# A graph network in one kernel: in the two relation passes, each row's three bf16 parts added up in PSUM by three narrow products instead of side by side by one wide one

## The reference, cut to what matters

```python
def _rgcn_conv(x, src, dst, edge_type, inv_deg, basis, comp, root, bias):
    xs = x[src]
    c = comp[edge_type]
    m = c[:, 0:1] * (xs @ basis[0])
    for b in range(1, basis.shape[0]):
        m = m + c[:, b:b + 1] * (xs @ basis[b])
    agg = jax.ops.segment_sum(m * inv_deg[:, None], dst, num_segments=n_nodes)
    return agg + x @ root + bias
...
deg = jnp.zeros((n_rel, n_nodes), jnp.float32).at[edge_type, dst].add(1.0)
inv_deg = 1.0 / jnp.maximum(deg[edge_type, dst], 1.0)
...
h = relu(_rgcn_conv(x, ..., basis1, comp1, root1, bias1))
return _rgcn_conv(h, ..., basis2, comp2, root2, bias2)
```

## Time and profile before

| | |
|---|---|
| median of 3 runs | 5605.86 us (5604.53 to 5606.44) |
| span of the profiled execution | 5606.0 us |
| instructions | 259126 |
| TensorE products busy | 4652.9 us, 83% |
| VectorE busy | 4578.9 us, 82% |
| ScalarE busy | 2971.1 us, 53% |
| first and second relation pass | about 905 and 897 us |
| granted TensorE clock, mean | 0.911 |

### The profile page before, as it was taken

The page is one execution under the profiler, slowest core; times in us unless marked ns, Lnnn a source line. Parts: engine busy times, 40 slices in busy tenths (PEclk is TensorE's granted clock), DMA queues, the critical chain, the costliest instruction groups (busy, mean ns, idle before and its releaser), DMA issues.

```text
span 5606.0 us, 259126 instructions
## 1 busy us (share of the span) xinstructions
PE 4652.9 (83%) x99331; PEld 3864.3 (69%) x99331; DVE 4578.9 (82%) x10121; ACT 2971.1 (53%) x9016; POOL 1075.8 (19%) x1785
## 2 busy tenths in 40 slices
PE   2566666666399999977996999979999998999998
PEld 1344433444299999977886999967777776777776
DVE  8999999999799999988888888886666666666665
ACT  2566656666132222227775333346666665666665
POOL 2455555555211111110000222210000000000000
PEclk7777777777699999988998999989999999999999
DMA  1000000000188888850001444433333333333332
GB/s 47 1 1 1 1 1 1 1 1 1 48 260 255 253 253 253 254 161 13 0 0 45 121 121 121 120 90 91 89 90 90 89 90 87 91 91 91 90 90 78
DMA packets 305217, 501.31 MB, mean 89 GB/s; under 512 B 76918, under 2 KB 78454, under 8 KB 305126
## 3 DMA queue, kind: packets, MB, share of 16 engines
q1 hardware_dynamic: 303782, 499.39, 30.7%
q0 software_dynamic: 576, 0.52, 0.0%
q10 hardware_dynamic: 768, 0.16, 0.0%
HBM read 408.40 MB, written 91.57 MB: 89 GB/s over the span
## 4 chain that ended last, share of the span: by engine, by line
PE 47%; DVE 27%; issue 17%; ACT 3%; POOL 3%; DVEq 1%; DMA 1%; ACTq 0%; POOLq 0%; another core or an unknown queue 0%; SPq 0%
PE PS L1415 17%; PE PS L1408 8%; DVE agg L1764 7%; PE PS L1211 6%; DVE arena L1728 5%; PE PS L1189 4%; PE PS L1191 4%; DVE Hp L1728 3%; DVE arena L1770 2%; POOL arena L737 2%; DVE tmp L1728 2%; ACT arena L971 2%; PE PS L1462 2%; PE PS L1206 2%; PE PS L1445 1%
## 5 line engine op out<-in xcount | busy, mean ns | idle before, releaser
L1728 DVE TENSOR_TENSOR arena<-iotab,arena 128x1024 bf16<-128x1024 bf16 (+6 forms) x1813 | 1741.5, 990 | 452.9 <-PE PS L1415 383.9
L971 ACT ACTIVATE arena<-PS 128x384 bf16<-128x384 f32 x2450 | 1069.2, 495 | 601.5 <-PE PS L1408 598.4
L1415 PE MATMUL PS<-arena 32*128 32x193 bf16 (+1 forms) x41552 | 1082.1, 243 | 7.6 <-issue 3.4
L808 ACT ACTIVATE arena<-PS,m 128x196 bf16<-128x196 f32 x1813 | 746.0, 431 | 547.3 <-POOLq L570 328.8
L1415 PEld LDWEIGHTS PS<-arena 32*128 32x128 bf16 x41552 | 815.8, 93 | 198.5 <-issue 166.1
L1077 PE MATMUL PS<-arena,tmp 128*128 128x262 bf16 x1813 | 504.7, 327 | 294.6 <-DVE tmp L1728 294.4
L1408 PE MATMUL PS<-Hp,arena 128*128 128x192 bf16 (+1 forms) x4900 | 644.4, 250 | 91.1 <-DVE Hp L1575 34.9
L1069 PE MATMUL PS<-agg,onesb 128*128 128x196 bf16 x1715 | 513.4, 301 | 202.9 <-ACT arena L808 198.5
L1070 PE MATMUL PS<-Hp,own_b 128*128 128x196 bf16 x1813 | 544.4, 304 | 55.8 <-DVE Hp L1728 54.5
L1408 PEld LDWEIGHTS PS<-Hp,arena 128*128 128x128 bf16 x4900 | 338.4, 99 | 304.5 <-issue 178.7
L1189 PE MATMUL PS<-Hp,arena 128*128 128x72 bf16 x7350 | 499.3, 198 | 44.0 <-DVE arena L2094 40.8
(11 more groups left out here) (362 smaller groups left out, 8170.2 us busy)
## 6 DMA issues: line engine op xcount, KB each, us to landing
arena<-hots SPq DMA_DIRECT2D x735, 256.0 KB, 2.6
arena<-codes SPq DMA_DIRECT2D x245, 512.0 KB, 5.2
hots<-arena SPq DMA_DIRECT2D x245, 256.0 KB, 5.2
arena<-hots SPq DMA_DIRECT2D x147, 320.0 KB
arena<-codes SPq DMA_DIRECT2D x49, 640.0 KB, 5.6
hots<-arena SPq DMA_DIRECT2D x49, 320.0 KB, 5.5
rows_h<-Hn SPq DMA_DIRECT2D x4, 1568.0 KB, 9.1
rows_l<-Y SPq DMA_DIRECT2D x1, 1764.0 KB, 10.4
```

The costliest lines, as they stand in the source:

```text
L808: act.activation(junk[:, j % 4, :], ps[j % 4][:, 0:KEYS], ACT.Relu, bias=m256[:, 0:1], accum_out=rank[:, j:j + 1]).then_inc(k_rank, 1)
L971: act.activation(RG[g % 2][:, 2 * i:2 * i + 2, 0:RW], ps[PAIR_BANK[q]][:, 0:2 * RW].rearrange("p (k c) -> p k c", k=2), ACT.Copy).then_inc ...
L1415: last = pe.matmul(ps[2 + q][:, b * SW:b * SW + SW - o], one_hot[32 * q:32 * q + 32, b * P:(b + 1) * P], rows_of[32 * q:32 * q + 32, 0:SW ...
L1728: return dve.tensor_tensor(to.rearrange("p k (n t) -> p k n t", t=4), iota_of[:, 0:n].rearrange("p (n t) -> p n t", t=4)[:, None, :, :] .t ...
```

## The change

`scatter_typed` makes, for each half `b`, three rounds of four products, one for each part `a` (2, 1, 0), all three into the same 64 columns, so that PSUM adds the parts up. Part 2 has the column of ones behind it (CV = DIM + 1 = 65 columns, 64 in the second pass). The sum of a half now takes 65 columns of a bank instead of 193. In `take_sums` the four reductions are gone: the multiplication reads the sums from PSUM and writes `Zs`. The semaphore `z_free` is gone, and TensorE's first scatter of a window waits for `z_s`, which the multiplication posts. In the first pass the reciprocal of the counts, which came after the release, now stands ahead of it.

```diff
                     def scatter_typed(one_hot, rows_of, starts, stops):
                         for b in range(2):
-                            for q in range(4):
-                                last = pe.matmul(ps[2 + q][:, b * SW:b * SW + SW - o],
-                                                 one_hot[32 * q:32 * q + 32, b * P:(b + 1) * P],
-                                                 rows_of[32 * q:32 * q + 32, 0:SW - o], start=(starts and b == 0),
-                                                 stop=(stops and b == 1))
+                            for a in (2, 1, 0):
+                                v = CV - o if a == 2 else DIM
+                                for q in range(4):
+                                    last = pe.matmul(ps[2 + q][:, b * CV:b * CV + v],
+                                                     one_hot[32 * q:32 * q + 32, b * P:(b + 1) * P],
+                                                     rows_of[32 * q:32 * q + 32, a * DIM:a * DIM + v],
+                                                     start=(starts and b == 0 and a == 2),
+                                                     stop=(stops and b == 1 and a == 0))
...
                         if i == 0 and g == 0:
-                            pe.wait_ge(z_free, dx + (o * WINDOWS + 1))
+                            if not is_zero(dx):
+                                pe.wait_ge(z_s, dx + o * WINDOWS)
...
-            for links in (3, 1, 4, 3, 2):
+            for links in (3, 1, 4, 3, 1):
...
                 def take_sums(dx):
                     dve.wait_ge(r_sum, dx + (o * WINDOWS + 1))
                     per = inv[:, bass.ds(dx, 1), :].rearrange("p w r -> p (w r)")
+                    sums = PS[:, 2 * 512:6 * 512].rearrange("p (q x) -> p q x", q=4)[:, :, 0:2 * CV] \
+                        .rearrange("p q (b x) -> p q b x", b=2)
                     if o == 0:
-                        met = PS[:, 2 * 512:6 * 512].rearrange("p (q x) -> p q x", q=4)[:, :, RW:RW + SW + 1:SW]
-                        dve.tensor_scalar(per.rearrange("p (q b) -> p q b", b=2), met, 1.0, None, ALU.max)
-                    for q in range(4):
-                        last = dve.tensor_reduce(Zs[:, 2 * q:2 * q + 2, :],
-                                                 ps[2 + q][:, 0:2 * SW].rearrange("p (b x) -> p b x", b=2)[:, :, 0:RW]
-                                                 .rearrange("p b (a c) -> p b c a", a=PARTS), AX.X, ALU.add)
-                    flink(last)
-                    dve.sem_inc(z_free, 1)
-                    if o == 0:
+                        flink(dve.tensor_scalar(per.rearrange("p (q b) -> p q b", b=2), sums[:, :, :, DIM], 1.0, None, ALU.max))
+                        dve.sem_inc(s_held, 1)
                         flink(dve.reciprocal(per, per))
-                    dve.tensor_tensor(Zs, Zs, bc(per, DIM), ALU.mult).then_inc(z_s, 1)
+                    dve.tensor_tensor(Zs.rearrange("p (q b) c -> p q b c", b=2), sums[:, :, :, 0:DIM],
+                                      bc(per.rearrange("p (q b) -> p q b", b=2), DIM), ALU.mult).then_inc(z_s, 1)
...
-                links = 3 - o
+                links = 3 - 2 * o
...
                         dve.memset(RG[0][:, :, RW:SW], 1.0)
-                        dve.memset(RG[1][:, :, RW:SW], 1.0).then_inc(z_free, 1)
-                        dve.sem_inc(z_done, 1)
+                        dve.memset(RG[1][:, :, RW:SW], 1.0).then_inc(z_done, 1)
```

More of the change, by code:

```diff
@@ L369, in gnn_stack @@
             "r_oh", "r_gath", "r_ev", "r_scat", "r_sum"))
-        z_free, z_s, z_hi, z_t, z_tc, z_out, z_done = (sem(n) for n in (
-            "z_free", "z_s", "z_hi", "z_t", "z_tc", "z_out", "z_done"))
+        z_s, z_hi, z_t, z_tc, z_out, z_done = (sem(n) for n in (
+            "z_s", "z_hi", "z_t", "z_tc", "z_out", "z_done"))
         q_load, q_idx, q_in, q_mm, q_ei, q_eo = (sem(n) for n in ("q_load", "q_idx", "q_in", "q_mm", "q_ei", "q_eo"))
```

## The result

The changed kernel takes **8331.39 us** (median of 4 runs, 8328.01 to 8334.88) against 5606.15 us (5604.53 to 5607.61, 4 runs): ratio 1.486, interval 1.484 to 1.488. It is slower by 2,725 us, 27.8 us for each of the 98 windows. The sign and the mechanism were forecast, the time was not: 8,331 us lies far above the range's 7,250.

The account below looks back on a forecast made before the run. TensorE's stream was taken to bound the two relation passes (1,802 of 5,606 us). Refetching code, +9.1 us a window over 98 windows, gave +890 us with the narrow products' +0.87 inside and sums 0: 6,500 us, range 5,670 to 7,250.

Parts of the forecast that it names:

- The sign and the mechanism: Whole kernel: slower (chance 0.89), because TensorE's longer loop body in the relation passes is fetched anew every turn, +890 us.
- Part 1's own price: TensorE's scatter: three narrow products for one cost +8.2 ns per group of four, +0.87 us a window, +85 us.
- The floor of 20 ns a product: Rival, TensorE's scatter: 20.5 ns a product is an issue limit whatever the columns, +1,680 us, 7,290 us; chance 0.04.
- The 25 ns: TensorE products: quoted minimum from start to start however few the columns; said to change nothing if it holds per group.
- Part 2: Sums on VectorE: four reductions removed, multiplication reads PSUM, banks free earlier; worth at most 8 us, counted as 0.
- off the path: ScalarE's `own_rows` and the next one-hots move ahead by over a microsecond, without shortening the window.
- Part 3, whether the code is kept: TensorE's relation loop: body 2.73 times as large, taken not to stay on chip; rival that it fits, 5,690 us, chance 0.17.
- Part 3, packets a turn: Instruction queue q8 in the relation loop: 10.9 packets a window and one for the jump back, 11.9.
- Part 3, the price of a packet: Instruction fetch in the relation loop: 2.3 us a packet, 27.4 us a window against 18.3, +890 us.
- Some 0.6 us from crossing to start: Past the old loop's end: time from the first instructions there to the packet's start, used as the delay before each fetch.
- The 2.4 us from a packet's start to its first instruction: Where TensorE plainly starves: packet starts at 3773.7, next load at 3776.12; used in the upper bound of a packet's period.
- its bounds, 1.6 to 3.0: Period of a fetched packet in us: 0.6 + 1.0 up to 0.6 + 2.4; at 3.0, 35.7 us a window, +1,705 us.

Follow-up runs that it names:

- e2: Kernel before with 16 of 53 blocks a window scattered by three narrow side-by-side products, sums as before: 5681.75 us, ratio 1.0121.
- e4: Changed kernel with only one of the three rounds of products, low and middle parts left out of the sums: 5244.66 us, ratio 0.934 to the kernel before.
- e1: Kernel before with every block scattered by three narrow products side by side into the old 193 columns, reductions and z_free kept: 8332.82 us, ratio 1.484.
- e8: Kernel before with only columns 128 to 192 scattered, four reductions over those read three times, z_free kept: 5297.91 us, ratio 0.9456.
- e6: Kernel before with 24 of 53 blocks a window scattered by narrow side-by-side products, sums as before: 6044.85 us, ratio 1.0785.
- e5: Kernel before, wide products and old sums, with three windows to a turn of TensorE's loop in the relation passes: 5809.80 us, ratio 1.0366.
- e3: Kernel before with 32 of 53 blocks a window scattered by narrow side-by-side products, sums as before: 7318.25 us, ratio 1.303.

## Why the prediction was wrong in size

**Part 1's own price: right.** +8.2 ns a group forecast, +8.1 measured where code is kept (e2). Products a window as forecast (1,339). The floor of 20 ns a product is out (7.5 ns in e4), and a group of four takes 30 ns or more. The 25 ns that the prediction quotes from the Trainium skill ("TensorE: Matmul & The Clock Gate", where they stand in the section "Wait — 56ns, not 53.3ns?") therefore bound nothing here; per product the trace is well below them.

**Part 2: right that it is no matter here**, with the reductions put back (e1) the ratio is the same within 0.2%. The multiplication from PSUM takes 692 ns (L2395), as forecast. But "off the path" holds only while TensorE or its feed is the bound: with slack on TensorE it is worth 64 us (e8 against e4), by the one-hots behind the reductions, which the prediction had only called off the path.

**Part 3, whether the code is kept: right.** It was given 0.68 to not fit. The ladder of 1,030, 1,540, 1,800, 2,050, 2,310 and 2,700 instructions shows it, the turns of e6 show it with one and the same body, and e5 shows how much hangs on what the fetching must keep up with: with more code than the changed kernel's, also fetched in every turn, but wide products behind it, 205 us are lost and not 2,725.

**Part 3, packets a turn: nearly.** 10.9 and one for the jump forecast, 12 in the first pass and 13 in the second measured.

**Part 3, the price of a packet: the step that failed.** The prediction took the middle, 2.3 us, between 0.6 + 1.0 and 0.6 + 2.4. Both choices in it were wrong.
- "Some 0.6 us from crossing to start", read at the end of the loop, was taken for the delay from entering a block to the next packet. In the starved loop that delay is 1.1 to 1.6 us, 1.4 at the place shown above.
- The 2.4 us from a packet's start to its first instruction was put down in part to q1's load of 91%. In the changed kernel the DMA engines stand at 0.15 and it is 2.3 to 2.9 all the same; at 5004.1, where nothing but q8 started a packet within 0.2 us, it is 2.7. The packet's own 0.9 to 1.3 us is about half of it or less.

1.4 + 2.4 = 3.8 us, outside what was called its bounds, 1.6 to 3.0. With it the prediction's own sum is 11.9 x 3.8 = 45.2 us a window (measured in the first pass 45.4, in the second, with 13 packets, 47.6) and (45.2 - 18.3) x 98 = +2,636: 8,242 us, 1.1% below the measured time. The mechanism held; one term was too small by 1.5 us and was paid twelve times a window.

Treating the one row of starvation as disturbed gave the middle of 2.3 in place of 3.0. The ceiling itself, 3.0, was too low because 0.6 stood in it for 1.4. The place of starvation had both halves: after the first load at 3776.12 the next packet of the kernel before starts at 3777.5 to 3777.6, 1.4 us later, and with the 2.4 us that is 3.8. The earlier trace rows could have warned of it too: straight code took a packet in some 4.6 us without loss, which allows any period up to that, so the range should have gone up to 4.6 us, 54.7 us a window, 9,170 us.

What stays open: how the 2.3 to 2.9 us from a packet's start to its use are made up beyond the packet's own 0.9 to 1.3, and why the fall of the granted clock to 0.6 went with it. The clock did not set the time: at 0.84 (e3) 251 packets moved in a millisecond, at 0.62 (e1) 266, not fewer.

No kernel here beats the kernel before by doing the whole work. One round of products did because it left two thirds of the columns out.

## What to carry to other kernels

Count the instructions of TensorE's loop body before splitting products: at about 1,540 it was kept on the chip here, at 1,800 it depended on where it lay, and from 2,050 on every turn fetched all of it at 3.8 to 4.0 us for 256 instructions, 15 ns each. Code that isn't kept costs little while the work behind each 256 instructions takes longer than that (wide products: 4.6 us), only some 7 us at the jump back; it sets the time when the work is shorter (narrow ones: 1.8 us, an estimate from 19.2 us of work for 10.5 packets). When idle time is put down to "issue" and no engine is near full, look at the packets of the instruction queue first.

## What the runs showed that was not expected

- The dearest stretch of the changed kernel has the DMA engines at 0.15: the fetch is slow by its delay (3.8 us for a packet that moves in 0.9 to 1.3), not by load.
- A body at the edge of the memory loses every other turn: 32.7 and 18.5 us in turn, 7 and 2 packets (e6).
- A jump back to code that is gone costs 6.95 us (e5), nearly two packets.
- Starved in bursts, TensorE was granted 0.58 to 0.63 of its clock; with the same narrow products and kept code it stayed at 1.00 (e2: 3930 to 4670 us).
